# A sort by one-hot matrices on one core: four engines' programs shifted by a column group, one-hots double-buffered, ranks folded

## The reference

```python
h = jnp.maximum(_layernorm(x, axis=-1), 0.0)
x = x + _L0_gnn_ref(h, src, dst, 6250)        # segment_sum(h[src], dst)
h = jnp.maximum(_layernorm(x, axis=-1), 0.0)
x = x + _L1_gnn_ref(h, ..., src, dst)         # three layers of gated messages over the same edges
return x
```

## Time and profile before

| | us |
|---|---|
| runs of the kernel (3), median | 4698.56 (4697.19 to 4701.59) |
| the profiled execution, its own time | 4695.09 |
| its span | 4693.4 |
| TensorE, VectorE, ScalarE, GpSimd busy in the span | 4160, 4005, 2568, 2387 |
| mean granted clock of TensorE | 0.94 |

### The profile page before, as it was taken

How to read it: one execution, slowest core, us unless ns; L and a number is a source line. 1 busy time by engine, 2 the same in 40 slices (tenths; PEclk the granted TensorE clock), 3 DMA queues, 4 the chain that set the end, 5 groups by cost and what they waited for, 6 DMA issues and landing times. The chain is left out here.

```text
span 4693.4 us, 254410 instructions
## 1 busy us (share of the span) xinstructions
PE 4160.4 (89%) x100368; PEld 3931.9 (84%) x100369; DVE 4004.9 (85%) x6206; ACT 2568.3 (55%) x4057; POOL 2387.4 (51%) x3439
## 2 busy tenths in 40 slices
PE   5888859999995999979998999979998899979997
PEld 5888848888884999968886899978887899978887
DVE  6666679999996788889997788889997788879998
ACT  4666649999992111157775111147776211137776
POOL 4555537777772222257775122247776222237776
PEclk7777769999997999989998999989999999989999
DMA  1000028999992677746662677746663577756664
GB/s 28 1 1 1 1 59 260 267 268 263 270 268 80 227 242 239 239 136 161 161 161 61 233 239 241 246 145 162 161 161 92 195 239 239 245 160 161 162 161 131
DMA packets 532061, 793.98 MB, mean 169 GB/s; under 512 B 66324, under 2 KB 466120, under 8 KB 531976
## 3 DMA queue, kind: packets, MB, share of 16 engines
q1 hardware_dynamic: 499048, 714.07, 48.2%
q0 software_dynamic: 32928, 78.72, 8.2%
HBM read 672.34 MB, written 120.24 MB: 169 GB/s over the span
## 5 line engine op out<-in xcount | busy, mean ns | idle before, releaser
L1113 PE MATMUL pre_ps<-rows_a,hotT_a 128*128 128x64 bf16 x21609 | 1287.1, 193 | 48.3 <-DMA hotT_a<-hot_scratch 27.3
L1342 POOL TENSOR_TENSOR message<-message,message_parts 128x448 f32<-128x448 f32 x1029 | 1100.8, 1070 | 438.7 <-ACT message_parts L1327 428.5
L1113 PE MATMUL pre_ps<-table,hotT_a 128*128 128x64 bf16 x21609 | 1288.0, 193 | 7.3 <-issue 7.3
L1113 PEld LDWEIGHTS pre_ps<-rows_a,hotT_a 128*128 128x128 fp8e4 x21609 | 1130.6, 98 | 56.0 <-issue 55.9
L1113 PEld LDWEIGHTS pre_ps<-table,hotT_a 128*128 128x128 fp8e4 x21609 | 1131.5, 98 | 7.9 <-issue 7.7
L1353 DVE TENSOR_TENSOR message_parts<-message,message_parts 128x448 bf16<-128x448 f32 x1029 | 943.0, 916 | 2.3 <-ACT message_parts L1318 2.1
L1193 DVE SCALAR_TENSOR_TENSOR weighed<-pre_ps,w 128x448 f32<-128x448 f32 x1029 | 643.1, 625 | 312.6 <-PE pre_ps L1113 220.4
L1280 PE MATMUL row_ps<-table,hot_b 128*128 128x64 bf16 x21609 | 803.6, 194 | 68.2 <-DMA hot_b<-hot_scratch 65.2
L1293 PE MATMUL sum_ps<-message_parts,hot_b 128*128 128x192 bf16 x7203 | 760.2, 245 | 89.2 <-DVE message_parts L1353 75.1
L1280 PEld LDWEIGHTS row_ps<-table,hot_b 128*128 128x128 fp8e4 x21609 | 756.9, 98 | 83.1 <-issue 82.9
L1327 ACT ACTIVATE message_parts<-message 128x448 bf16<-128x448 f32 x1029 | 594.6, 578 | 419.5 <-DVE message L1368 419.3
(11 more groups left out here) (148 smaller groups left out, 5718.9 us busy)
## 6 DMA issues: line engine op xcount, KB each, us to landing
hotT_a<-hot_scratch SPq DMA_DIRECT2D x1029, 224.0 KB, 4.6
hot_b<-hot_scratch SPq DMA_DIRECT2D x1029, 224.0 KB, 2.6
hot_scratch<-hot SPq DMA_DIRECT2D x343, 336.0 KB, 6.0
hot_a<-hot_scratch SPq DMA_DIRECT2D x147, 784.0 KB, 5.1
places<-slots_scratch POOLq DMA_DIRECT2D x686, 112.0 KB, 5.8
out<-res SPq DMA_DIRECT2D x1, 1536.0 KB
slots_scratch<-bins SPq DMA_DIRECT2D x49, 12.5 KB
raw<-in_src SPq DMA_DIRECT2D x1, 768.0 KB
```

What stands on the lines that cost most here:

```text
L1113: last = nc.tensor.matmul(pre_ps[g][:, j, :], hotT[:, b, g, end, j * P:(j + 1) * P].bitcast(FP8), table, start=end + part == 0, stop=end = ...
L1342: pool.tensor_tensor(message[:, g, :, :], message[:, g, :, :], parts[:, g, :, 0, :], ALU.subtract).then_inc(s["rest_ready"], 1)
```

## The change

The one-hot tile `hot_w` has two buffers. With that, each engine's program is moved by a row in parts: TensorE adds the ranks of row c, counts for row c + 1, then scatters row c - 1; VectorE picks the ranks of c first, writes the one-hots of c + 1, the spread of c - 1 and the values of c last; ScalarE and GpSimd fetch and widen the blocks two rows ahead and the places one row ahead, in functions of their own. `block_wide` and `place_wide` have one buffer for two. A new VectorE operation adds the two halves of `picked_w` (`folded_w`), and 26 rank matmuls read that for 49. The one-hots are 52 wide for 50, and the value tile has its two halves at columns 0 and 64 of 128, cleared once at the start, so the scatter's weights are 128 columns for 100 and the bins 128 rows. GpSimd reads `starts` four times a row for twice. The reader of the bins takes the second half from row 64.

```diff
     k.CAP = cap
-    k.NBP = k.NB + 1
+    k.NBP = (k.NB // 4 + 1) * 4
+    k.HALF = P // 2
...
-        block_wide = sb("block_wide", [P, 2, WIN, NBP], BF16)
-        place_wide = sb("place_wide", [P, 2, WIN, NBP], BF16)
+        block_wide = sb("block_wide", [P, WIN, NBP], BF16)
+        place_wide = sb("place_wide", [P, WIN, NBP], BF16)
         rank_wide = sb("rank_wide", [P, 2, WIN, P], BF16)
-        hot = sb("hot_w", [P, COLS, GROUPS, NBP], BF16)
-        value = sb("value_w", [P, 2, WIN, 2 * NBP], BF16)
+        hot = sb("hot_w", [P, 2, COLS, GROUPS, NBP], BF16)
+        value = sb("value_w", [P, 2, WIN, 2 * HALF], BF16)
...
+        folded = sb("folded_w", [P, WIN, NBP // 2], BF16)
         spread = sb("spread", [P, WIN, P], BF16)
-        bins = sb("bins", [2 * NBP, 2, P], U8)
+        bins = sb("bins", [2 * HALF, 2, P], U8)
         sooner_ps = [ps(f"sooner_ps{i}", [P, GROUPS, NBP]) for i in range(2)]
         rank_ps = [ps(f"rank_ps{i}", [P, WIN]) for i in range(2)]
-        bins_ps = [ps(f"bins_ps{i}", [2 * NBP, P]) for i in range(2)]
...
-                def fetch(c, b, step):
+                def fetch_key(c, b, step):
                     at = bass.ds(pool.value_load(k.starts[0:1, bass.ds(c, 1)]), WIN)
                     step(pool.tensor_copy(key_w[:, :], k.key[:, at]))
-                    pool.tensor_copy(place_w[:, b, :, :], k.place1[:, :, at])
                     step(pool.tensor_scalar(local[:, b, :], key_w[:, :], base[:, 0:1], None, ALU.subtract))
+                    pool.sem_inc(s["keyed"], 1)
                     step(pool.tensor_scalar(base[:, :], base[:, :], float(BLOCK_KEY), None, ALU.add))
-                    pool.sem_inc(s["fetched"], 1)
+                def fetch_places(c, b, step):
+                    at = bass.ds(pool.value_load(k.starts[0:1, bass.ds(c, 1)]), WIN)
+                    step(pool.tensor_copy(place_w[:, b, :, :], k.place1[:, :, at]))
+                    pool.sem_inc(s["placed"], 1)
+                def clear_spills(c, b, step):
+                    at = bass.ds(pool.value_load(k.starts[0:1, bass.ds(c, 1)]), WIN)
...
+                    clear_spills(c, b, step)
+                    wait_count(pool, s, s["twins_ready"], c + 3)
+                    fetch_key(c + 2, b, step)
                     wait_count(pool, s, s["values_ready"], c + 2)
-                    fetch(c + 1, 1 - b, step)
+                    wait_count(pool, s, s["places_wide"], c + 2)
+                    fetch_places(c + 1, 1 - b, step)
                     if not first:
                         note_spills(c - 1, 1 - b, step)
...
                 def add_ranks(c, b):
-                    pe.wait_ge(s["picked"], c + 3)
+                    pe.wait_ge(s["folded"], c + 3)
...
-                    for n in range(NB):
-                        nc.tensor.matmul(rank_ps[b][:, :], k.identb[:, :], by_column[1][:, :, n], start=n == 0, stop=False,
+                    for n in range(NBP // 2):
+                        nc.tensor.matmul(rank_ps[b][:, :], k.identb[:, :], folded[:, :, n], start=n == 0, stop=False,
                                          skip_group_check=True)
...
                 def row(c, b, nth, first):
-                    count_sooner(c, b)
                     add_ranks(c, b)
+                    count_sooner(c + 1, 1 - b)
                     if not first:
                         scatter(c - 1, 1 - b)
+                count_sooner(0, 0)
                 each_row(pe, NB, row)
                 scatter(NB - 1, 0)
...
+                def widen_blocks(c, b):
+                    act.wait_ge(s["keyed"], c + 3)
+                    act.wait_ge(s["hot_ready"], c + 2)
+                    nc.scalar.activation(block_wide[:, :, :], local[:, b, :].unsqueeze(2).to_broadcast([P, WIN, NBP]),
                                          ACT.Copy).then_inc(s["blocks_wide"], 1)
-                    act.wait_ge(s["values_ready"], c + 1)
-                    nc.scalar.activation(place_wide[:, b, :, :], place_w[:, b, 0, :].unsqueeze(2).to_broadcast([P, WIN, NBP]),
+                def widen_places(c, b):
+                    act.wait_ge(s["placed"], c + 3)
+                    act.wait_ge(s["values_ready"], c + 2)
+                    nc.scalar.activation(place_wide[:, :, :], place_w[:, b, 0, :].unsqueeze(2).to_broadcast([P, WIN, NBP]),
                                          ACT.Copy).then_inc(s["places_wide"], 1)
+                def take_prefix(c, b):
+                    act.wait_ge(s["prefixed"], c + 3)
+                    act.wait_ge(s["picked"], c + 1)
+                    nc.scalar.activation(sooner[:, b, :, :], sooner_ps[b][:, :, :], ACT.Copy).then_inc(s["prefix_ready"], 1)
                 def take_bins(c, b, nth):
                     act.wait_ge(s["scattered"], c + 3)
...
                 def row(c, b, nth, first):
-                    act.wait_ge(s["prefixed"], c + 3)
-                    act.wait_ge(s["picked"], c + 1)
-                    nc.scalar.activation(sooner[:, b, :, :], sooner_ps[b][:, :, :], ACT.Copy).then_inc(s["prefix_ready"], 1)
-                    widen(c + 1, 1 - b)
...
+                    take_prefix(c + 1, 1 - b)
+                    widen_blocks(c + 2, b)
+                    widen_places(c + 1, 1 - b)
                     if not first:
                         take_bins(c - 1, 1 - b, nth if b == 1 else nth - 1)
-                widen(0, 0)
+                widen_blocks(0, 0)
+                widen_blocks(1, 1)
+                widen_places(0, 0)
+                take_prefix(0, 0)
...
+                def pick_blocks(c, b):
                     dve.wait_ge(s["blocks_wide"], c + 3)
-                    dve.wait_ge(s["prefixed"], c + 2)
-                    dve.wait_ge(s["picked"], c + 2)
-                    dve.wait_ge(s["values_ready"], c + 2)
-                    nc.vector.tensor_tensor(by_column[0], k.number[:, 0:NBP].unsqueeze(1).to_broadcast([P, WIN, NBP]),
-                                            block_wide[:, b, :, :], ALU.is_equal).then_inc(s["hot_ready"], 1)
-                    dve.wait_ge(s["fetched"], c + 3)
+                    dve.wait_ge(s["prefixed"], c + 1)
+                    dve.wait_ge(s["picked"], c + 1)
+                    dve.wait_ge(s["values_ready"], c + 1)
+                    nc.vector.tensor_tensor(by_column[:, b, :, :], k.number[:, 0:NBP].unsqueeze(1).to_broadcast([P, WIN, NBP]),
+                                            block_wide[:, :, :], ALU.is_equal).then_inc(s["hot_ready"], 1)
...
+                def set_values(c, b):
                     dve.wait_ge(s["hot_ready"], c + 3)
+                    dve.wait_ge(s["placed"], c + 3)
                     dve.wait_ge(s["scattered"], c + 1)
-                    nc.vector.tensor_tensor(value[:, b, :, NBP:2 * NBP], by_column[0],
+                    nc.vector.tensor_tensor(value[:, b, :, HALF:HALF + NBP], by_column[:, b, :, :],
                                             place_w[:, b, 1, :].unsqueeze(2).to_broadcast([P, WIN, NBP]), ALU.mult)
                     dve.wait_ge(s["places_wide"], c + 3)
-                    nc.vector.tensor_tensor(value[:, b, :, 0:NBP], by_column[0], place_wide[:, b, :, :], ALU.mult)\
+                    nc.vector.tensor_tensor(value[:, b, :, 0:NBP], by_column[:, b, :, :], place_wide[:, :, :], ALU.mult)\
                         .then_inc(s["values_ready"], 1)
+                def pick_ranks(c, b):
                     dve.wait_ge(s["prefix_ready"], c + 3)
-                    dve.wait_ge(s["ranked"], c + 2)
-                    nc.vector.tensor_tensor(picked[:, :, :, :], hot[:, :, :, :],
+                    dve.wait_ge(s["folded"], c + 2)
+                    nc.vector.tensor_tensor(picked[:, :, :, :], hot[:, b, :, :, :],
                                             sooner[:, b, :, :].unsqueeze(1).to_broadcast([P, COLS, GROUPS, NBP]), ALU.mult)\
                         .then_inc(s["picked"], 1)
+                    dve.wait_ge(s["picked"], c + 3)
+                    dve.wait_ge(s["ranked"], c + 2)
+                    nc.vector.tensor_tensor(folded[:, :, :], picked_cols[:, :, 0:NBP // 2], picked_cols[:, :, NBP // 2:NBP],
+                                            ALU.add).then_inc(s["folded"], 1)
+                def spread_out(c, b):
+                    dve.wait_ge(s["ranks_wide"], c + 3)
+                    dve.wait_ge(s["scattered"], c + 2)
+                    nc.vector.tensor_tensor(spread[:, :, :], k.number[:, :].unsqueeze(1).to_broadcast([P, WIN, P]),
+                                            rank_wide[:, b, :, :], ALU.is_equal).then_inc(s["spread"], 1)
+                def row(c, b, nth, first):
+                    pick_ranks(c, b)
+                    pick_blocks(c + 1, 1 - b)
                     if not first:
                         spread_out(c - 1, 1 - b)
+                    set_values(c, b)
+                nc.vector.memset(value[:, :, :, :], 0.0).then_inc(s["step"], 1)
+                dve.wait_ge(s["step"], 1)
```

(18 more changed lines are left out.)

51 lines of the change are left out of this document (28 added, 23 removed).

## The result

| | before | after |
|---|---|---|
| median of the runs taken together, us | 4699.0 | 4725.07 (4722.95 to 4725.92) |
| ratio to before, 95% interval | | 1.0055 [1.0042, 1.0067] |
| the profiled execution, its own time | 4695.09 | 4722.95 |
| its span | 4693.4 | 4721.3 |
| first pick, last pick, end of the last `spread` | 45.70, 616.71, 628.23 | 48.14, 639.38, 654.23 |

Slower by 26 us, 0.55%. The forecast was 4702 with a likeliest range of 4690 to 4715, and 4735 as the upper end for the slower rival; so the sum pointed the right way and was too small: +3.3 us for some 26. The measured time lies beyond the likeliest range, nearer to the slower rival's time than to the forecast. The chances pointed the other way, with 0.38 for faster and 0.27 for slower. Of the 27.9 us between the spans 26.0 are the sort.

The account below looks back on a forecast made before the run. The prediction saw a TensorE ring bounding the sort before (row 11.9 us) and GpSimd after (7.5 work plus 4.6 blocking, 12.1). With start and tail that added 3.3 us to 4698.56, giving 4702; its own range 4690 to 4715.

Parts of the forecast that it names:

- slower rival: Sort: GpSimd's two-tensor operations wait out two VectorE operations, row 12.7 or 12.8 us, time 4735; chance 0.15.
- the sum: Whole kernel: sort rows at GpSimd's pace plus start and tail, +3.3 us on 4698.56, giving 4702.
- A ring through TensorE: Sort before the change: standing still 1.7, ranks 3.5, scatter 3.4, count 2.7 make an 11.3 us row; mean 11.9.
- VectorE's 8.9: Sort after the change: VectorE's operations, including the new fold at 0.6, add up to 8.9 us a row.
- The memset: Sort's start: clearing the value tile takes 4.0 us, hidden in VectorE's 4.98 us wait before its first `hot`.
- GpSimd's price: Sort after the change: GpSimd full, 7.5 us of work and 4.6 of blocking, sets a row of 12.1.
- the signs for the single operations: Profile after: GpSimd's `spill`, `key_w` or `inside` would show 1 to 2.5 us each.
- the blocking: Sort after the change: GpSimd's SBUF operations come out only behind VectorE's two-tensor operations, 4.6 us a row.
- The layout: One sort row timed from `local` written at 0: `spill` out 6.0, pick 10.4, fold's end 12.1, `local` 12.2.
- Gets through sooner: Sort: GpSimd slips in at VectorE's handovers, row 8.9 us at best, time 4555 (halfway 4627); chance 0.27.
- Held up in turn: Sort: ten short GpSimd operations, 2.8 us, delay VectorE, row 11.7 us, time 4689; chance 0.06.
- Waits out two: Sort: `spill` updates and squaring of `inside` wait out two VectorE operations, row 12.7 or 12.8, 4735; chance 0.15.

Follow-up runs that it names:

- b1: Kernel before, in its old order, with only the value tile made 128 wide and cleared at the start: 4706.79 us, ratio 1.0015.
- f0: Kernel before plus 30 unused matmuls of constants on TensorE between count and ranks, where it stood idle: 4614.49 us, ratio 0.9827.
- b2: Kernel before, in its old order, with only the fold and 26 rank matmuls for 49, one-hots 52 wide: 4703.92 us, ratio 1.0009.
- b3: Kernel before, in its old order, with fold, 26 rank matmuls and 128-wide value tile, so the change without reordering: 4702.65 us, ratio 1.0011.
- a1: Changed kernel without GpSimd's spill bookkeeping (six of ten SBUF operations, two of four loads) and ScalarE's wait for it: 4552.83 us, ratio 0.9699.
- a2: Changed kernel without ScalarE's wait for `noted`; VectorE copies the 36 ranks GpSimd reads into a small tile: 4717.69 us, ratio 1.0040.
- a3: Changed kernel with three GpSimd register loads for four and the spill clearing moved to the end of its row: 4719.27 us, ratio 1.0042.
- n1: Changed kernel with spill bookkeeping mostly on VectorE, GpSimd keeping five of ten operations: five runs at 4558 to 4568 us, four at 4644 to 4649.
- o1: Kernel before with only the new order and double-buffered one-hots; no fold, 49 rank matmuls, value tile 100 wide: 4705.72 us, ratio 1.0020.

## Why the prediction was right or wrong, point by point

**What bounds the kernel: right in name, wrong in cause.** A ring through TensorE it is. But I read its 3.42 us of scatter as the price of loading 100 columns of weights, and took a saving down to 2.0 for the wide tile. b1 has 3.43 with the wide tile, f0 2.19 with the narrow one: the pace is 107 ns a matmul at 1.2 GHz and 56 ns at full clock (start to start, both widths). The view that says so, stretches with their granted clock cut at the matmul groups, I had read only for the sort as a whole, where it says 0.78. Nor did shortening the ranks open the ring, as b2 showed. My ring had TensorE's pieces in it and left out a second one, VectorE's value, pick and `spread` closed by the scatter. Before, that one comes to 10.4 by its own rows (3.19, 1.02, 2.55, 0.1 to the scatter, 3.52; an estimate), so the ranks hid 1.1 us at most; the fold and the wider operands lengthen it to the 11.4 that b3 shows.

**The sums.** VectorE's 8.9: right, a1 runs at 8.86 with three engines as in the change. The fold 0.65 for 0.6, `spread` 2.54, value 2.16 and 1.14. TensorE: ranks 1.86 and 0.28 as said; the scatter 2.17 inside its bounds but by the clock. The memset took 3.90 for 4.0 but was not hidden: it started at 36.81 only, and the first one-hot follows its end at 40.74, 1.0 later than the 39.76 of the earlier trace rows. From there to the first pick it takes 7.4 us for 5.9, with 4.10 for 2.75 us in the count's 30 matmuls; I had 0.8 for both together, and they cost 2.4.

**GpSimd's price: right, and the heart of it.** Forecast: a row of 12.1 with GpSimd full, 7.5 of work and 4.6 of blocking. The measured row splits into the same 7.5 (4.7 idle and 2.8 for ten operations at their short lengths) and 5.1 of blocking. `rank_wide` was to wait 3 to 4 us and waits 2.5; `block_wide` waits 2.2; VectorE was to idle some 3 us and idles 3.7. Of the signs for the single operations, `spill` at 2.4 us and `inside` at 1.35 came, the key copy has 0.58. Taking GpSimd's bookkeeping away gives VectorE's row (a1); taking one wait away gives 0.1 us a row (a2), one load nothing (a3).

**Its size, the step that was off: the blocking, 5.1 us for 4.6.** The layout, from `local` at 0, against the row that starts at 413.78: `spill` out 6.0, measured 6.03; `inside` 8.0 and 9.2, measured 8.16 and 9.15; pick 10.4, measured 10.64; fold's end 12.1, measured 12.46; `local` 12.2, measured 12.70. So no wait was missed; the handovers were. GpSimd to ScalarE took 0.16 and the rest up to the pick 0.08; the fold waits for its own pick, 1.17 after its start for my 1.1; the fold is 0.05 longer; `local` comes out 0.24 behind it for my 0.1. Those are 0.5 us. A slip of my own comes on top: the layout ends with `local` at 12.2, and that is the row, but I closed it at 12.1. By my own layout the sum would have been 4 us more, about 4706. The mean row is 12.65, so 0.55 above the forecast, and in 43 rows that is 23.6 us, as much as the 23 by which 4725 passes 4702. The rest of the sort nearly cancels: first pick 1.6 late, tail 0.85 longer, and 3 less for one more early row at 9.

**The rivals.** *Gets through sooner*: did not happen in the change; n1's shorter pattern is what it looks like. *Held up in turn*: not in the way that it was meant. `spread` took 2.54 to 2.55 us with `spill` blocked behind it all along. But where a blocked operation came out just after the start of a VectorE operation, that one was some 0.05 us longer: in f0 `spread` took 2.61 us in the 39 rows where it happened and 2.55 in two where it did not, and in before L492 took 1.14 for the 1.08 of the earlier trace rows. That is about 0.1 us a row, which the sum put at nothing. The Trainium skill (SBUF — State Buffer, Who interferes with whom) has contention only as an exclusive lock of the shared ports, by issue order; here the blocked side was GpSimd in each of these rows. *Waits out two*: its time, 4735, was nearest, and that is chance, since its mechanism is absent: `spill` came out behind `spread` alone and the squaring L343 behind one value operation, and even `local` behind the fold alone. Its row of 12.7 was met by other means.

**The ends and the rest.** The building and the layers were counted as unchanged: they differ by 1.9 us in sum.

## What to carry to other kernels

Where a trace shows short GpSimd operations that take 0.2 us alone and 2 us beside VectorE, count GpSimd by where its operations fall among VectorE's, not by their own length: filling VectorE's gaps takes away the places where they came out, and saving a load or a wait between two such places gave 0.1 us of 12.65 at most here. Cut the stretch table at the groups of matmuls before explaining a matmul's length, since a gap of 1.8 us in TensorE cost 1.2 to 1.9 us of the scatter two steps later. And before cutting an engine's work, check that the ring has no second path of nearly the same length.

## What the runs showed of the hardware

**Full clock bought by useless matmuls.** 1.83 us of matmuls on constants in a gap of 1.8 us held the granted clock at 1.00 in all but two rows between 64 and 540 us (those two took 11.25 us for 10.2); the same gap left open let it fall to 0.50 over all or most of the scatter in every row. In o1, with other gaps, the fall never met the scatter, which took 2.19 us there with the tile 100 wide. The Trainium skill (TensorE: Matmul & The Clock Gate, What's actually happening) has throttled as the default, released by activity; f0 agrees, 0.966 granted over the whole span for 0.94.

**Width of the weights.** The load itself is shorter with 128 columns (141 ns for 194 in the mean of the scatter, 98 for 127 where the clock was full, in the changed kernel and in f0), the matmul stream is not. The Trainium skill (TensorE: Matmul & The Clock Gate, Weight-path perf modes — Fast Weight Load (FWL) and DoubleRow) turns the fast load on at 128 weights that are not FP32; the durations agree, but with 128 moving columns behind each load no time came of it.

**A blocked GpSimd operation can be passed over.** Most came out 0.1 to 0.2 us after the VectorE operation beside them, also when the next followed at once. In one pattern of n1 the same copy stayed in for 5.6 us and was passed over by two or three of them, which were as long as elsewhere (2.54, 2.10 and 1.12 us). What decides between the two stays open.
